# Second stage of layer two: the centre and weight products of two steps issued in one run

## The chip, the cores and the metric

The kernel runs on one core of a Trainium2 chip. The metric is the device time of one execution in microseconds (us), lower is better. All engine names are those of the profile: PE is TensorE's matmul, PEld its weight load, DVE is VectorE, ACT is ScalarE, POOL is GpSimd and SP is SyncE, which here only issues DMAs.

## The reference, cut to what matters

The input has 4 images of 64 channels and 256 x 256 pixels. Layer one is a gated convolution with a blockwise Fourier part. Layer two runs a linear state-space recurrence over all pixels, once row by row and once column by column, each with its own weights:

```
fx  = layer_norm(x, ln1_g, ln1_b)
h   = s5_scan(fx, ...)              # forward and backward scan, complex state
x   = gelu(h) + fx
fx2 = layer_norm(x, ln2_g, ln2_b)
y   = fx2 @ ff_enc.T @ ff_dec.T + fx2
out = fusion_w @ concat(y_h, y_v) + fusion_b
```

The change touches only the part from `gelu(h)` on. A second layer norm is needed there: its mean is taken out by a product with a centring matrix, its variance comes from the squares of that, and the product with the weight matrix (in which `ff_enc`, `ff_dec` and the fusion are folded) is scaled afterwards by the reciprocal deviation.

## The kernel before, in words

The work on an image is layer one, then for layer two each direction in turn (`d` = 1, then `d` = 0) a first stage (`pa_...`) and a second stage (`pb_...`). So the second stage runs 8 times. It goes through 16 groups (`NG`) of 4 steps, 64 steps `m` in all (`M`), each over a tile of 128 x 512. Each engine has its own written-out program with its own loop over `m`, and semaphores tie them together.

In one step TensorE does, in this order (`pb_pe`, the loop at its end):

- `first(m)`: 12 matmuls (L1776), into the PSUM bank of the step.
- in the second step of a group (m % 4 == 1) `var`: 32 short matmuls (L1350) that add up the squares of the group before.
- `bc(m - 6)`: one matmul (L1821) that spreads the reciprocal deviations of six steps ago (`LAG`) over the partitions. It alternates between banks 3 and 5, and so waits for the `norm` of two steps before it.
- `second(m)`: 6 matmuls (L1789) from the state `XP`, into the bank of `first`. In the first step of a group it waits for the new `XP` (semaphore `X`). There is one `XP`, so VectorE can write it only when the last `second` of the old group has ended.
- `center(m - 1)`: two fp32 products with `ctq` (L1800) into bank 2 and two with `Wq` (L1803) into bank 6 or 7, each on a 64 x 64 quadrant of the array, so that the four run side by side. Each is recorded as two passes.

ScalarE (`pb_act`) does the Gelu of the step from PSUM to `X2` (L1865), then the square of the centred values (L1871) and the copy of the weight product into `tW` (L1878). In m % 4 == 1 it also takes the square root of the variances (L1854), with two table loads around it, and in `d` = 0 it puts out rows together (L1753).

VectorE (`pb_dve`) does `deviations_b` in m % 4 == 1 (L1340 to L1345: reciprocal and the tile `RD` that `bc` reads), then `add(m)` (L1922: fx times gain plus Gelu, into `X2`, the operand of `center`), in m % 4 == 3 `parts` (L1908 and L1911: the new `XP`), then `norm(m - 6)` (L1929: the spread deviations times `tW`), then `scan` of the next group in m % 4 == 0 (L1899 and four tiny operations) and `rotate` in m % 4 == 1 and 2 (L1719, L1720, L1722).

GpSimd (`fin_v` L1731, `fin_h` L1741) adds each normed tile to the tile `av` or `ah` from memory. It starts when `norm` has ended.

SyncE issues all loads and stores in one queue. Near the end of `d` = 0 it already issues the first loads of the next image, the tiles `XT` among them.

Of the kernel before, what the change touches and what calls it, by code (L numbers as in the profile page):

```python
# [7 lines left out]
ALU = mybir.AluOpType  # L8
ACT = mybir.ActivationFunctionType
# [5 lines left out]
NG = 16  # L15
# [3 lines left out]
M = 4 * NG  # L19

PARTS = ((0, 0), (0, 1), (1, 0))
LAG = 6
NW = 8
# [87 lines left out]
def build(nc, a, NB):  # L111
# [34 lines left out]
    g1 = at("g1", [128, 2])  # L146
# [143 lines left out]
    ah = [at(f"ah{i}", [128, 2, 1024]) for i in range(2)]  # L290
    oh = at("oh", [128, 8, 256])
    XT = [at(f"XT{i}", [128, 512]) for i in range(3)]

    ps = [nc.alloc_psum_tensor(f"ps{i}", [128, 512], F32) for i in range(6)]
    ps67 = nc.alloc_psum_tensor("ps6", [128, 2, 512], F32)
# [1336 lines left out]
    def pb_sp(e, b, d):  # L1632
        f = phase(b, d)

        def load(n):
            e.wait_ge(sem["yd"], M * f + 4 * (n - 2) + 4)
            e.dma_start(fq[n % 2][1][:].rearrange("p a b -> p (a b)").bitcast(F32), fl_d[b, d, order[n]]
                        ).then_inc(sem[f"fl_in{n % 2}"], 16)
            e.wait_ge(sem["x2"], M * f + 4 * (n - 2) + 4)
            e.dma_start(fi[n % 2][:].rearrange("p a b -> p (a b)"), fx_d[b, d, order[n]]).then_inc(sem[f"fi_in{n % 2}"], 16)  # L1640

        def load_v(n):
            if n >= 2:
                e.wait_ge(sem[f"avs{n % 2}"], 16 * (8 * b + (n - 2) // 2 + 1))
            for p, hf in ((0, slice(64, 128)), (1, slice(0, 64))):
                e.dma_start(av[n % 2][hf].rearrange("c v h w -> c (v h w)"),
                            x1v_d[b, order[n], p].rearrange("c v h w -> c (v h w)")).then_inc(sem[f"av{n % 2}"], 16)

        def load_h(n):
            g = order[n]  # L1650
            for p in range(2):
                if n >= 2:
                    e.wait_ge(sem["il"], M * b + 4 * (n - 2) + 2 * p + 2)
                for v, hf in ((0, slice(64, 128)), (1, slice(0, 64))):
                    e.dma_start(ah[n % 2][hf, p, :].rearrange("c (k r) -> c k r", k=16),
                                acc_d[b, :, 1 - p, :, v, 8 * g:8 * g + 8, :].rearrange("k c h w -> c k (h w)")
                                ).then_inc(sem[f"ah{n % 2}"], 16)

        e.wait_ge(sem["bm"], 32 * (f + 1))
        for p in range(2):  # L1660
            e.dma_start(Cwr[:, p, :].bitcast(F32), kc_d[d, p, :, 1024:2048]).then_inc(sem["kC"], 16)
        e.wait_ge(sem["t"], M * (f + 1))
        e.dma_start(TBo[:].rearrange("p a b -> p (a b)"), tb_d[d, :, 1024:2048]).then_inc(sem["kTo"], 16)
        if d:
            load_v(0)
            load_v(1)
        else:
            for k in range(2):
                e.wait_ge(sem[f"avs{k}"], 16 * 8 * (b + 1))
            load_h(0)  # L1670
            load_h(1)
        for n in range(NG + 1 if d else NG + 2):
            if 2 <= n + 2 < NG:
                load(n + 2)
            if n == NG - 1:
                if d:
                    ahead_a(e, b, 0)
                elif b + 1 < NB:
                    ahead_0(e, b + 1)
            if d and n:  # L1680
                g = order[n - 1]
                e.wait_ge(sem["finv"], M * b + 4 * n)
                e.dma_start(acc_d[b, g].rearrange("p c v h w -> (p c) (v h w)"),
                            av[(n - 1) % 2][:].rearrange("p v h w -> p (v h w)")).then_inc(sem[f"avs{(n - 1) % 2}"], 16)
                if n + 1 < NG:
                    load_v(n + 1)
            if not d and n >= 2:
                if n < NG:
                    load_h(n)
                if n == NG - 1 and b + 1 < NB:  # L1690
                    load_xt(e, b + 1, 1)
                    load_raw(e, b + 1, 1)
                    load_xt(e, b + 1, 2)
                    load_raw(e, b + 1, 2)
                if n < NG or b + 1 == NB:
                    store_rows(e, b, n - 2)
                elif n == NG:
                    for t in range(3):
                        load_h_rows(e, b + 1, t)
        if b == NB - 1 and not d:  # L1700
            e.wait_ge(sem["ost"], 32 * NG * NB)
# [53 lines left out]
    def pb_pe(e, b, d):  # L1755
        f = phase(b, d)

        def bank(m):
            return ps[{2: 3, 3: 5}.get(m, m % 2)]

        def first(m):
            n, s = divmod(m, 4)
# [29 lines left out]

        def center(m):
            e.wait_ge(sem["x2"], M * f + m + 1)
            if m:
                e.wait_ge(sem["sr"], M * f + m)
            if m >= 2:
                e.wait_ge(sem["tw"], M * f + m - 1)
            for hf in (slice(0, 64), slice(64, 128)):
                ins = e.matmul(ps[2][hf, :], ctq[hf, hf], X2[m % 2][hf, :], start=True, stop=True)  # L1800
            ins.then_inc(sem["cc"], 1)
            for hf, other in ((slice(0, 64), slice(64, 128)), (slice(64, 128), slice(0, 64))):
                ins = e.matmul(ps[6 + m % 2][other, :], Wq[hf, hf], X2[m % 2][hf, :], start=True, stop=True)  # L1803
            ins.then_inc(sem["w"], 1)

        def var(n):
# [6 lines left out]
        def bc(m):  # L1813
            n, s = divmod(m, 4)
            if s == 0:
                e.wait_ge(sem["rsb"], NG * f + n + 1)
            if m >= 2:
                e.wait_ge(sem["n2"], M * f + m - 1)
            else:
                e.wait_ge(sem["gl"], M * f + m + 3)  # L1820
            e.matmul(ps[3 + 2 * (m % 2)][:], Bc[:, 512 + 128 * s:640 + 128 * s], RD[:], start=True,  # L1821
                     stop=True).then_inc(sem["bd"], 1)

        for m in range(4):
# [1 line left out]
        for m in range(M + LAG):  # L1826
            if 4 <= m < M:
                first(m)
            if m >= 5 and m % 4 == 1 and m <= M + 1:
                var(m // 4 - 1)  # L1830
            if m >= LAG:
                bc(m - LAG)
            if m < M:
                second(m)
            if 1 <= m <= M:
                center(m - 1)

    def pb_act(e, b, d):
# [9 lines left out]
        for m in range(M + 2 if d else M + 9):  # L1848
# [11 lines left out]
                    p1(e, b + 1, 0)  # L1860
            if m < M:
                e.wait_ge(sem["y"], M * f + m + 1)
                if m >= 2:
                    e.wait_ge(sem["w"], M * f + m - 1)
                e.activation(X2[m % 2][:], ps[{2: 3, 3: 5}.get(m, m % 2)][:], ACT.Gelu_apprx_tanh, bias=cD[:, 4 * d + s:4 * d + s + 1]  # L1865
                             ).then_inc(sem["gl"], 1)
            if 1 <= m <= M:
                e.wait_ge(sem["cc"], M * f + m)
                if m >= 5:
                    e.wait_ge(sem["va"], M * f + m - 4)  # L1870
                e.activation(sr[:, (m - 1) % 4, :], ps[2][:], ACT.Square, bias=cC[:, d:d + 1]).then_inc(sem["sr"], 1)  # L1871
                e.wait_ge(sem["w"], M * f + m)
                if m - 1 >= NW:
                    if d:
                        e.wait_ge(sem["finv"], M * b + m - NW)
                    else:
                        e.wait_ge(sem["finh"], M * b + m - NW)
                e.activation(tW[:, (m - 1) % NW, :], ps[6 + (m - 1) % 2][:], ACT.Identity, bias=cW[:, d:d + 1]  # L1878
                             ).then_inc(sem["tw"], 1)
            if s == 1 and n:  # L1880
                for i in range(4):
                    part(n + 1, i)
# [5 lines left out]
    def pb_dve(e, own, b, d):  # L1888
# [25 lines left out]
        def add(m):  # L1914
            n, s = divmod(m, 4)
            e.wait_ge(sem["gl"], M * f + m + 1)
            if s == 0:
                if n >= 2:
                    fi_there(e, f, n)
                else:  # L1920
                    e.wait_ge(sem["nn"], M * (f + 1))
            e.scalar_tensor_tensor(X2[m % 2][:], fi[n % 2][:, s, :], g1[:, d:d + 1], X2[m % 2][:], ALU.mult, ALU.add  # L1922
                                   ).then_inc(sem["x2"], 1)

        def norm(m):
            e.wait_ge(sem["bd"], M * f + m + 1)
            e.wait_ge(sem["tw"], M * f + m + 1)
            t = tW[:, m % NW, :]
            e.tensor_tensor(t, ps[3 + 2 * (m % 2)][:], t, ALU.mult).then_inc(sem["n2"], 1)  # L1929

        e.wait_ge(sem["badd"], NG * (f + 1))
        e.wait_ge(sem["baddd"], f + 1)
# [4 lines left out]
        for m in range(M + 8):  # L1937
            n, s = divmod(m, 4)
            if s == 1 and 1 <= n <= NG:
                deviations_b(e, own, f, n - 1, "se", NG * f + n, "rsb")  # L1940
            if m < M:
                add(m)
                if s == 3 and n + 1 < NG:
                    parts(n + 1)
            if m >= LAG and m - LAG < M:
                norm(m - LAG)
            if s == 0 and n + 1 < NG:
                scan(n + 1)
            if s in (1, 2) and n + 1 < NG:
# [151 lines left out]
```

## Time and profile before

| | |
|---|---|
| time, median of 3 runs | 9187.77 us (9186.68 to 9197.3) |
| time of the profiled execution | 9189.68 us |
| its span | 9187.9 us |
| mean granted TensorE clock | 0.968 |
| PE busy | 8467.4 us, 92% |
| DVE busy | 8000.4 us, 87% |
| ACT busy | 5173.3 us, 56% |
| POOL busy | 1604.8 us, 17% |

The profile records one execution. Busy shares are means over very different stages, so what sets the pace of the second stage has to be read from a stretch inside it. The second stages start at about 1493 us for the first image and end at about 9163 us for the last one; the stretches used here lie in the last two images. Matmuls are pipelined: a matmul of 512 columns is recorded with some 0.39 us, but the next one starts some 0.23 us after it.

### The profile page before, as it was taken

To read this page: it belongs to the slowest core of one execution; us is meant where nothing else is said; L and a number is where in the kernel's file an instruction comes from. 1 tells how busy PE (TensorE), PEld (TensorE's weight loads), DVE (VectorE), ACT (ScalarE), POOL (GpSimd) and SP (SyncE) were. 2 spreads that over 40 slices of the span, in tenths; PEclk is the share of its full clock that TensorE was granted. 3 is DMA by queue.
4 is the path that set the end of the run, shared out by engine and by line. 5 is a ranking of instruction groups with operands and counts; after the bars stand their busy time and mean duration, and the time that the engine had idled before them with its cause. 6 is when DMAs were issued, how large, how long until landed. Compare 5 with 4: busy or idle time off the path is not lost. (4 is left out here: it accounts for less than half of the span.)

```text
span 9187.9 us, 202861 instructions
## 1 busy us (share of the span) xinstructions
PE 8467.4 (92%) x82258; PEld 5525.6 (60%) x82258; DVE 8000.4 (87%) x11203; ACT 5173.3 (56%) x8027; POOL 1604.8 (17%) x1834
## 2 busy tenths in 40 slices
PE   0899989999899998998989999899998999899998
PEld 0566655656566664665656666565565666556565
DVE  7799988888799998879869999887887999898886
ACT  0455555576655556556765554656675555555666
POOL 0000003333300001232320000223341000023333
PEclk9899999999999998999999999999999999999999
DMA  4789876585688887557569887846667878765855
GB/s 113 173 189 197 188 195 205 175 259 152 169 188 192 188 196 224 165 179 240 168 166 196 190 191 167 256 157 213 197 178 158 179 171 179 178 208 182 258 150 156
DMA packets 1370028, 1719.03 MB, mean 187 GB/s; under 512 B 849788, under 2 KB 1081356, under 8 KB 1283852
## 3 DMA queue, kind: packets, MB, share of 16 engines
q1 hardware_dynamic: 1369100, 1706.04, 72.3%
q8 instruction: 657, 10.76, 0.5%
q14 instruction: 271, 2.22, 0.1%
HBM read 852.77 MB, written 514.86 MB: 149 GB/s over the span
## 5 line engine op out<-in xcount | busy, mean ns | idle before, releaser
L1181 DVE SCALAR_TENSOR_TENSOR F<-U,LW,F 106x512 f32<-106x512 f32 x2048 | 1537.2, 751 | 63.5
L1776 PE MATMUL ps<-fp,Dwr 128*128 128x512 f32 x6144 | 1548.8, 401 | 1.6 <-DVE tt L1544 1.6
L1776 PEld LDWEIGHTS ps<-fp,Dwr 128*128 128x128 f32 x6144 | 1115.2, 188 | 617.6 <-ACT x L1865 289.6
L1048 ACT ACTIVATE xr<-P 64x1024 fp32r<-64x1024 f32 x512 | 542.9, 1060 | 780.7 <-issue 770.6
L1865 ACT ACTIVATE x<-ps,cst 128x512 f32<-128x512 f32 x512 | 351.8, 687 | 1038.7 <-PE ps L1789 1034.2
L871 PE MATMUL ps<-P,WP 128*128 128x512 f32 x3072 | 859.9, 416 | 52.6 <-DMA H<-P 50.9
L1789 PE MATMUL ps<-XP,Cwr 128*128 128x512 f32 x3072 | 805.5, 399 | 82.2 <-DVE XP L1911 82.2
L871 PE MATMUL ps<-H,WP 128*128 128x512 f32 x3072 | 819.9, 402 | 0.0
L871 PEld LDWEIGHTS ps<-P,WP 128*128 128x128 f32 x3072 | 567.0, 191 | 391.5 <-issue 206.9
L1922 DVE SCALAR_TENSOR_TENSOR x<-fx,g,x 128x512 f32<-128x512 f32 x512 | 382.9, 748 | 467.3 <-ACT x L1865 467.0
L1424 PE MATMUL ps<-fp,Bwr 128*128 128x512 f32 x3072 | 774.9, 403 | 0.4 <-DVE tt L1544 0.3
L1741 POOL TENSOR_TENSOR ah<-tW,ah 128x256 f32<-128x256 f32 x512 | 584.4, 1167 | 992.2 <-DVE tW L1929 991.6
L1789 PEld LDWEIGHTS ps<-XP,Cwr 128*128 128x128 f32 x3072 | 585.0, 192 | 229.5 <-issue 96.7
L1424 PEld LDWEIGHTS ps<-fp,Bwr 128*128 128x128 f32 x3072 | 581.7, 193 | 218.7 <-issue 98.1
L1098 POOL TENSOR_SCALAR xo<-xo 64x512 f32<-64x512 f32 x4 | 6.0, 1500 | 4042.0 <-DVE xo L1206 4042.0
L871 PEld LDWEIGHTS ps<-H,WP 128*128 128x128 f32 x3072 | 577.7, 188 | 156.3 <-issue 1.9
L1731 POOL TENSOR_TENSOR av<-tW,av 128x512 f32<-128x512 f32 x256 | 473.5, 1855 | 1101.5 <-DVE tW L1929 1101.5
L1800 PE MATMUL ps<-x,ctq 64*64 64x512 f32 x2048 | 551.0, 615 | 10.2 <-DVE x L1922 10.0
L1803 PE MATMUL ps<-x,Wq 64*64 64x512 f32 x2048 | 551.0, 615 | 0.0
L1004 ACT ACTIVATE xh<-ps 128x504 f32<-128x504 f32 x256 | 151.1, 590 | 703.7 <-PE ps L820 703.5
L1157 DVE TENSOR_TENSOR Z<-ps,LW 128x680 f32<-128x680 f32 x512 | 441.4, 862 | 96.4 <-PE ps L835 88.5
L1462 ACT ACTIVATE sq<-ps,gn 128x512 f32<-128x512 f32 x512 | 350.1, 684 | 222.8 <-PE ps L1383 222.8
(302 smaller groups left out, 16726.8 us busy)
## 6 DMA issues: line engine op xcount, KB each, us to landing
H<-P SPq DMA_DIRECT2D x512, 585.0 KB, 7.4
raw<-x SPq DMA_DIRECT2D x240, 640.0 KB, 9.5
fx_d<-fx SPq DMA_DIRECT2D x112, 1024.0 KB, 6.6
fl_d<-fp SPq DMA_DIRECT2D x112, 1024.0 KB, 6.9
fp<-fl_d SPq DMA_DIRECT2D x112, 1024.0 KB, 6.7
fx<-fx_d SPq DMA_DIRECT2D x112, 1024.0 KB, 5.4
XT<-xT SPq DMA_DIRECT2D x256, 256.0 KB, 7.5
x1h_d<-xo SPq DMA_DIRECT2D x256, 256.0 KB, 9.2
```

What stands on the lines that cost most here:

```text
L871: e.matmul(ps[2 + i][:], w(pw_, W_CONV + 128 * j, 128), m, start=(j == 0 and pw_ == 0 and px == 0), stop=False)
L1048: ins = e.activation(xr[t % 2][hf], src, ACT.Copy)
L1157: e.tensor_tensor(Z[t % 2][:, 4 * h:4 * h + 4, :].rearrange("q (j p) h -> q j (p h)", j=2), ps67[:, :, 0:2 * HID], Wt.unsqueeze(1).to_broa ...
L1181: ins = e.scalar_tensor_tensor(o, u, wd[0:106, i:i + 1], o, ALU.mult, ALU.add)
L1424: ins = e.matmul(o[:], Bwr[:, w, 128 * (2 * s + j):128 * (2 * s + j) + 128], fp[g % 2][x][:, s, :], start=(s == 0 and w == 0 and x == 0), ...
L1731: e.tensor_tensor(o, t, o, ALU.add).then_inc(sem["finv"], 1)
L1741: ins = e.tensor_tensor(o, t, o, ALU.add)
L1776: ins = e.matmul(bank(m)[:], Dwr[:, w, c:c + 128], fq[n % 2][x][:, s2, :], start=(s2 == 0 and w == 0 and x == 0), stop=False)
L1789: ins = e.matmul(bank(m)[:], Cwr[:, w, c:c + 128], XP[x][:, j, :], start=False, stop=(j == 1 and w == 1))
L1800: ins = e.matmul(ps[2][hf, :], ctq[hf, hf], X2[m % 2][hf, :], start=True, stop=True)
L1803: ins = e.matmul(ps[6 + m % 2][other, :], Wq[hf, hf], X2[m % 2][hf, :], start=True, stop=True)
L1922: e.scalar_tensor_tensor(X2[m % 2][:], fi[n % 2][:, s, :], g1[:, d:d + 1], X2[m % 2][:], ALU.mult, ALU.add).then_inc(sem["x2"], 1)
```

## The change

`center(m)` is no longer called in every step. In every second step it is called twice in a row, after `second(m)`, for m - 2 and m - 1. For this the centred values get two banks (2 and 5), `X2` gets four buffers (the two new ones share their memory with `XT1` and `XT2`), and `bc` keeps only bank 3, so that it waits for the `norm` of the step before it. ScalarE does its squares and copies of two steps in a row as well. VectorE calls `norm` ahead of `add` and `parts`, no longer behind them. SyncE loads the `XT` tiles that share memory one iteration later, behind a wait for the last weight product.

```diff
+    X2 += XT[1:3]
...
                 if n == NG - 1 and b + 1 < NB:
+                    load_raw(e, b + 1, 1)
+                    load_raw(e, b + 1, 2)
+                if n == NG and b + 1 < NB:
+                    e.wait_ge(sem["w"], M * (f + 1))
                     load_xt(e, b + 1, 1)
-                    load_raw(e, b + 1, 1)
                     load_xt(e, b + 1, 2)
-                    load_raw(e, b + 1, 2)
...
         def bank(m):
-            return ps[{2: 3, 3: 5}.get(m, m % 2)]
+            return ps[{2: 3, 3: 4}.get(m, m % 2)]
...
         def center(m):
             e.wait_ge(sem["x2"], M * f + m + 1)
-            if m:
-                e.wait_ge(sem["sr"], M * f + m)
             if m >= 2:
+                e.wait_ge(sem["sr"], M * f + m - 1)
                 e.wait_ge(sem["tw"], M * f + m - 1)
             for hf in (slice(0, 64), slice(64, 128)):
-                ins = e.matmul(ps[2][hf, :], ctq[hf, hf], X2[m % 2][hf, :], start=True, stop=True)
+                ins = e.matmul(ps[(2, 5)[m % 2]][hf, :], ctq[hf, hf], X2[m % 4][hf, :], start=True, stop=True)
...
         def bc(m):
-            if m >= 2:
-                e.wait_ge(sem["n2"], M * f + m - 1)
+            if m:
+                e.wait_ge(sem["n2"], M * f + m)
             else:
-                e.wait_ge(sem["gl"], M * f + m + 3)
-            e.matmul(ps[3 + 2 * (m % 2)][:], Bc[:, 512 + 128 * s:640 + 128 * s], RD[:], start=True,
+                e.wait_ge(sem["gl"], M * f + 3)
+            e.matmul(ps[3][:], Bc[:, 512 + 128 * s:640 + 128 * s], RD[:], start=True,
                      stop=True).then_inc(sem["bd"], 1)
...
-            if 1 <= m <= M:
+            if m % 2 == 0 and 2 <= m <= M:
+                center(m - 2)
                 center(m - 1)
...
     def pb_act(e, b, d):
-            if 1 <= m <= M:
-                e.wait_ge(sem["cc"], M * f + m)
+            for c in (m - 2, m - 1) if m % 2 == 0 and 2 <= m <= M else ():
+                e.wait_ge(sem["cc"], M * f + c + 1)
...
     def pb_dve(e, own, b, d):
+            if m >= LAG and m - LAG < M:
+                norm(m - LAG)
             if m < M:
                 add(m)
                 if s == 3 and n + 1 < NG:
                     parts(n + 1)
-            if m >= LAG and m - LAG < M:
-                norm(m - LAG)
```

## Rows read from the trace of the kernel before

**Rows 1.** Chain that ended last, one group: start, us, what.
```profile
8404.00 2.98 PE ps L1776 x12
...
8408.57 0.58 PE ps L1800 x2
...
8409.59 2.97 PE ps L1776 x12
...
8423.73 1.01 PE ps L1350 x32
...
8427.57 0.66 PE ps L1776 x2
```

**Rows 2.** Timeline of PE, runs with no change of shape: start, us, engine, what.
```profile
7460.03 1.04 PE L898 MATMUL ps<-raw,FR 64*64 64x512 f32 x4
7460.89 1.05 PE L951 MATMUL ps<-F,LW 42*64 42x512 f32 x4
...
8169.18 5.60 PE L1776 MATMUL ps<-fp,Dwr 128*128 128x512 f32 x24
```

**Rows 3.** Timeline of ACT and DVE from the last `second` of a group.
```profile
8414.20 0.69 ACT L1865 ACTIVATE x<-ps,cst 128x512 f32<-128x512 f32 x1 [3.31 <-PE ps L1789]
...
8414.92 0.75 DVE L1922 SCALAR_TENSOR_TENSOR x<-fx,g,x 128x512 f32<-128x512 f32 x1 [0.24 <-ACT x L1865]
...
8416.26 1.29 DVE L1911 TENSOR_TENSOR XP<-tq,XP 128x512 fp32r<-128x512 f32 x2
```

**Rows 4.** Timeline where `second` waits for `XP`, early in a stage.
```profile
8204.85 1.28 DVE L1911 TENSOR_TENSOR XP<-tq,XP 128x512 fp32r<-128x512 f32 x2
...
8206.18 1.66 PE L1789 MATMUL ps<-XP,Cwr 128*128 128x512 f32 x6 [0.41 <-DVE XP L1911]
...
8207.77 0.65 PE L1800 MATMUL ps<-x,ctq 64*64 64x512 f32 x2
```

**Rows 5.** Timeline of DVE beside POOL's final addition, in both directions.
```profile
8406.74 2.03 POOL L1731 TENSOR_TENSOR av<-tW,av 128x512 f32<-128x512 f32 x1 [6.72 <-DVE tW L1929]
...
8407.17 2.13 DVE L1720 TENSOR_TENSOR tq<-S,TBo 128x512 f32<-128x512 f32 x1
...
8992.30 1.80 POOL L1741 TENSOR_TENSOR ah<-tW,ah 128x256 f32<-128x256 f32 x1
...
8993.84 0.28 DVE L1616 SCALAR_TENSOR_TENSOR S<-S,e,tiny 64x1 f32<-64x1 f32 x1
```

**Rows 6.** Whole run by source line: count, duration in ns, min/median/max.
```profile
L1616 DVE SCALAR_TENSOR_TENSOR S<-S,e,tiny x128: 218/219/276, 1508.5 to 9112.4; 64x1 f32<-64x1 f32 x128
...
L1720 DVE TENSOR_TENSOR tq<-S,TBo x256: 681/1373/2159, 1509.6 to 9121.3; 128x512 f32<-128x512 f32 x128
...
L1922 DVE SCALAR_TENSOR_TENSOR x<-fx,g,x x512: 736/751/754, 1518.9 to 9148.4; 128x512 f32<-128x512 f32 x171
...
L1731 POOL TENSOR_TENSOR av<-tW,av x256: 1567/1660/2692, 1546.8 to 8570.7; 128x512 f32<-128x512 f32 x128
```

**Rows 7.** Timeline from `var` to VectorE's `add`, and that `add` mid-stage.
```profile
8211.74 1.08 PE L1350 MATMUL ps<-sr,En 128*32 128x128 f32 x32
...
8215.59 0.74 DVE L1922 SCALAR_TENSOR_TENSOR x<-fx,g,x 128x512 f32<-128x512 f32 x1
...
8405.31 0.74 DVE L1922 SCALAR_TENSOR_TENSOR x<-fx,g,x 128x512 f32<-128x512 f32 x1
```

**Rows 8.** Timeline of PE and DVE at the end of a second stage.
```profile
8563.91 1.40 PE L1821 MATMUL ps<-RD,Bc 128*128 128x512 f32 x2 [3.76 <-DVE RD L1345]
...
8566.81 1.99 PE L1383 MATMUL ps<-xin,Mb 64*64 64x512 f32 x8
...
8563.77 0.68 DVE L1929 TENSOR_TENSOR tW<-ps,tW 128x512 f32<-128x512 f32 x1
...
8564.74 1.29 DVE L1929 TENSOR_TENSOR tW<-ps,tW 128x512 f32<-128x512 f32 x2 [0.29 <-PE ps L1821]
```

**Rows 9.** Timeline of SP's queue at the turn to another image.
```profile
6948.56 42.34 SPq L719 DMA_DIRECT2D H<-P  x6
```

More of the change, by code:

```diff
@@ L1794, in center @@
             e.wait_ge(sem["x2"], M * f + m + 1)
-            if m:
-                e.wait_ge(sem["sr"], M * f + m)
             if m >= 2:
+                e.wait_ge(sem["sr"], M * f + m - 1)
                 e.wait_ge(sem["tw"], M * f + m - 1)
             for hf in (slice(0, 64), slice(64, 128)):
-                ins = e.matmul(ps[2][hf, :], ctq[hf, hf], X2[m % 2][hf, :], start=True, stop=True)
+                ins = e.matmul(ps[(2, 5)[m % 2]][hf, :], ctq[hf, hf], X2[m % 4][hf, :], start=True, stop=True)
             ins.then_inc(sem["cc"], 1)
             for hf, other in ((slice(0, 64), slice(64, 128)), (slice(64, 128), slice(0, 64))):
-                ins = e.matmul(ps[6 + m % 2][other, :], Wq[hf, hf], X2[m % 2][hf, :], start=True, stop=True)
+                ins = e.matmul(ps[6 + m % 2][other, :], Wq[hf, hf], X2[m % 4][hf, :], start=True, stop=True)
             ins.then_inc(sem["w"], 1)
@@ L1862, in pb_act @@
                 e.wait_ge(sem["y"], M * f + m + 1)
-                if m >= 2:
-                    e.wait_ge(sem["w"], M * f + m - 1)
-                e.activation(X2[m % 2][:], ps[{2: 3, 3: 5}.get(m, m % 2)][:], ACT.Gelu_apprx_tanh, bias=cD[:, 4 * d + s:4 * d + s + 1]
+                if m >= 4:
+                    e.wait_ge(sem["w"], M * f + m - 3)
+                e.activation(X2[m % 4][:], ps[{2: 3, 3: 4}.get(m, m % 2)][:], ACT.Gelu_apprx_tanh, bias=cD[:, 4 * d + s:4 * d + s + 1]
                              ).then_inc(sem["gl"], 1)
-            if 1 <= m <= M:
-                e.wait_ge(sem["cc"], M * f + m)
[L1869 to L1873, printed above, removed]
+            for c in (m - 2, m - 1) if m % 2 == 0 and 2 <= m <= M else ():
+                e.wait_ge(sem["cc"], M * f + c + 1)
+                if c >= 4:
+                    e.wait_ge(sem["va"], M * f + c - 3)
+                e.activation(sr[:, c % 4, :], ps[(2, 5)[c % 2]][:], ACT.Square, bias=cC[:, d:d + 1]).then_inc(sem["sr"], 1)
+                e.wait_ge(sem["w"], M * f + c + 1)
+                if c >= NW:
                     if d:
-                        e.wait_ge(sem["finv"], M * b + m - NW)
+                        e.wait_ge(sem["finv"], M * b + c - NW + 1)
                     else:
-                        e.wait_ge(sem["finh"], M * b + m - NW)
-                e.activation(tW[:, (m - 1) % NW, :], ps[6 + (m - 1) % 2][:], ACT.Identity, bias=cW[:, d:d + 1]
-                             ).then_inc(sem["tw"], 1)
+                        e.wait_ge(sem["finh"], M * b + c - NW + 1)
+                e.activation(tW[:, c % NW, :], ps[6 + c % 2][:], ACT.Identity, bias=cW[:, d:d + 1]).then_inc(sem["tw"], 1)
             if s == 1 and n:
@@ L1921, in add @@
                     e.wait_ge(sem["nn"], M * (f + 1))
-            e.scalar_tensor_tensor(X2[m % 2][:], fi[n % 2][:, s, :], g1[:, d:d + 1], X2[m % 2][:], ALU.mult, ALU.add
+            e.scalar_tensor_tensor(X2[m % 4][:], fi[n % 2][:, s, :], g1[:, d:d + 1], X2[m % 4][:], ALU.mult, ALU.add
                                    ).then_inc(sem["x2"], 1)
@@ L1928, in norm @@
             t = tW[:, m % NW, :]
-            e.tensor_tensor(t, ps[3 + 2 * (m % 2)][:], t, ALU.mult).then_inc(sem["n2"], 1)
+            e.tensor_tensor(t, ps[3][:], t, ALU.mult).then_inc(sem["n2"], 1)
         e.wait_ge(sem["badd"], NG * (f + 1))
```

## Prediction

> **What bounds the kernel now.** I read the page first (PE is busy 92% and DVE 87%, so neither can be ruled out), then the list of waits, then the chain that ended last in a stretch in the middle of a second stage. There the chain consists of PE alone: each group of four steps takes 8427.57 - 8404.00 = 23.57 us, a plain step 8409.59 - 8404.00 = 5.59 us, and `center` 8409.59 - 8408.57 = 1.02 us of it [rows 1]. So a group is 4 x 5.59 + 1.21 us, the last for `var` and its surroundings. The reader should see that nothing outside PE appears in that chain, so what PE saves is saved, until something else comes late. Last I read the timeline of all engines in the same stretch, to find what is nearly late.
>
> **What PE saves.** A matmul with no change of shape around it costs (5.60 - 0.39) / 23 = 0.227 us [rows 2]. The 19 full-array matmuls of a step would be 4.32 us in one unbroken run; the step without `center` takes 4.57 us, and `center` itself 1.02 us, while a pair of fp32 passes of the same shape that follows another 64 x 64 product takes 7460.89 - 7460.03 = 0.86 us [rows 1, 2]. So going into the quadrant shape and back costs (4.57 - 4.32) + (1.02 - 0.86) = 0.41 us. Two `center` calls in one run have this once and not twice. I take 0.40 us for a pair. The bounds are 0.25 us (only the change on the side of `first` goes away) and 0.41 us. A group has two pairs: -0.80 us.
>
> **What becomes late: `XP`.** The pairs are issued in steps with even m, so after m % 4 == 3 no `center` stands between the last `second` of a group and the next group's `first`. It was the cover of a chain on other engines: that last `second` ends (8414.16), Gelu starts 8414.20, `add` 8414.92, `parts` ends 8417.55 [rows 3]. From end to end this is 3.39 us, and it can't begin sooner, since `XP` is single. Before, PE had `center`, `first` and `bc` meanwhile, 1.02 + 2.97 + 0.23 = 4.22 us. Now it has 13 matmuls, 13 x 0.227 = 2.95 us. Where `second` has to wait for `XP`, the following `center` starts 8207.77 - 8206.13 = 1.64 us after `parts` ended [rows 4]. So it would start 3.39 + 1.64 = 5.03 us after the last `second`, where an unbroken run brings it after 19 x 0.227 = 4.32 us, less 0.05 us of pipelining. The new stall is 0.76 us in each group (bounds 0.65 and 0.85). It eats the saving nearly whole: -0.04 us.
>
> **What is late next: `add` behind GpSimd.** `norm` now stands ahead of `add`, and GpSimd's final addition starts as soon as `norm` ends. The rows show that GpSimd's addition and a VectorE operation with two operands from SBUF exclude each other: L1720 takes 0.68 us alone, but 2.13 us when it starts inside the addition that began at 8406.74, so that it works as if it had begun 0.15 us before that addition's end [rows 5, 6]. Does this hold for `add`, a SCALAR_TENSOR_TENSOR? It never met an addition before (736 to 754 ns in all 512 cases), but a tiny operation of its kind took 0.28 us and not 0.22 where it started 0.26 us before the end of an addition (8994.10; 276 ns is also its maximum) [rows 5, 6]. I take it that `add` is held. The Trainium skill says the same in SBUF — State Buffer, section SBUF: two separate sides: the port pair that VectorE and GpSimd share is an exclusive lock, taken for a whole instruction by a VectorE operation with two SBUF inputs or by GpSimd, whoever starts first. The trace agrees for L1720 (2.13 against 0.68 us); for `add` the rule speaks against this change. By the sums below a group would be 24.33 us with it and 23.53 us without.
>
> Where are they in the critical step? Let z be the end of a group's first `second`. Then come two `center` (1.88 us) and `first` (2.97), so `var` starts at z + 4.85. VectorE gets through the deviations 8215.59 - 8211.74 = 3.85 us later [rows 7], at z + 8.70. From there to the end of the second `rotate` it was 8414.68 - 8405.31 = 9.37 us with the same operations in it [rows 3, 7] (the scan before it may get faster, since GpSimd has moved away from it, but it then waits for `var`). So `norm` of the last step runs from z + 18.07 to z + 18.75 and GpSimd's addition (1.66 us, [rows 6]) to z + 20.4. The last `second` ends three steps and `var` after z, that is 3 x 5.59 + 1.21 - 3 x 1.02 + 2 x 1.88 - 0.23 = 18.45 us; with Gelu, `add` could start at z + 19.2. It is held for about 1.1 us in this direction. In the other one there are two shorter additions for one, VectorE has less to wait for in `rotate`, and I expect 0.5 us. Mean: 0.80 us. Bounds: 0 (no hold, or the addition is over in time) and 1.5 us (`add` escapes, and `parts` is held). It goes in full into the stall of `second`.
>
> **A group**: 23.57 - 0.80 + 0.76 + 0.80 = 24.33 us, +0.76. There are 14 such groups in a stage (in the first, PE waits for VectorE anyway, and after the last no new `XP` is made) and 8 stages: 112 x 0.76 = +85 us.
>
> **The ends of a stage.** At the start, `center` of step 2 ran while PE would have waited for `XP` [rows 4]; now it follows: +0.86 us. One more pair near the end saves 0.40 us. At the end the last four `bc` follow each other; with one bank each waits for the `norm` before it. It was 8566.81 - 8563.91 = 2.90 us from the first of them to the next stage's product. Now the first goes at 8564.51 (end of the `norm` that starts at 8563.77, plus 0.06), and each further one 0.83 + 0.68 + 0.06 = 1.57 us later, so the next stage starts 0.60 + 3 x 1.57 + 0.70 - 2.90 = 3.1 us later [rows 8]. That is in full at the four turns between directions. At the turn to another image the copies H<-P wait for SyncE's queue until 6948.56 and PE for them [rows 9], and at the end of the kernel GpSimd, with 1.66 us an addition [rows 6] against 1.57 us from `norm` to `norm`, sets the pace: 1 us each is my estimate, four times. Sum: 8 x (0.86 - 0.40) + 4 x 3.1 + 4 x 1 = +20 us.
>
> **Costed at nothing.** The later `XT` loads: in SyncE's queue they stand ahead of H<-P as before, and the last weight product is done when the queue gets there. Were that cover gone, it would be a few us at three turns. The moved squares and copies on ScalarE (56% busy) end before `var`. The single bank of `bc` inside a group: each `norm` ends at least 0.8 us before its `bc`; without that margin each us late is paid once a group, 112 us. The second Gelu bank for step 3 only changes a number.
>
> **Sum.** 9189.68 (the profiled execution, 1.9 us above the median) + 85 + 20 = 9295, so 9293 us beside the median.
>
> **Rivals.** *The stall without the hold*: `add` is not held, or GpSimd is done in time. For it: no row shows `add` itself held. Against it: the tiny operation of the same kind. Then 112 x -0.04 + 20 = +16: 9204 us; with a saving of 0.25 us a pair +50: 9238 us. Chance 0.17. *The saving comes through* (faster): the wait for `XP` is hidden. It decides at the point where `parts` ends less than 2.6 us after the last `second`, for instance if Gelu and `add` cost PE nothing because `first` takes longer than I say; against it stand the 3.39 us read directly. Then 8 x 29 x -0.40 + 20 = -73: 9115 us; half of it 9150. Chance 0.10. *One bank for `bc` is too few*: VectorE, held more often by GpSimd, becomes the pace of a group, and `bc` waits for `norm` in mid-group. For it: DVE had only 0.24 us idle before `add` in the critical step [rows 3]. Then a group takes 25 us or more: 112 x 1.5 + 20 = +188: 9376 us. Chance 0.10. *The change does nothing that can be measured* is contained in the first rival's lower part.
>
> **Numbers.** My forecast has a chance of 0.63, and its own range is 9250 to 9330. A measurement of this kernel tells about 0.2% (18 us) from no change. Faster by more: 0.10. Within: 0.11, from the first rival. Slower by more: 0.79. The range for 8 in 10 goes down into the first rival and up to a hold of 1.5 us: 9197 to 9345.
>
> **What the profile after would show.** Right: PE's `second` in the first step of a group has idle time before it, released by L1911, some 1.5 us 14 times a stage; L1922 has a maximum near 1.5 to 2 us, no longer 754 ns; the scan L1899 loses its long cases (near 2.8 us); the group is near 24.3 us; two `center` in a row take 1.88 us. Wrong: if L1922 keeps its 0.75 us, the hold is wrong; if no idle time stands before `second`, the stall is; if a pair takes 2.04 us, the saving is; if `bc` has idle time released by L1929 in mid-group, the third rival is right.

## The result, and the profile after

The changed kernel takes 9299.12 us (median of 4 runs, 9296.88 to 9302.09) against 9190.8 us before in the same comparison (9186.68 to 9197.3): a ratio of 1.0116, 95% interval 1.01 to 1.0132. The forecast was 9293 us. The profiled execution took 9298.31 us, 108.6 us more than the one of before.

The page of the changed kernel, its engines and one of the costliest groups (line numbers have moved by one to three; behind the first bar stand busy us and mean ns of one, behind the second the idle time before and its releaser):

```profile
PE 8401.1 (90%) x82258; PEld 5561.6 (60%) x82258; DVE 7967.6 (86%) x11203; ACT 5148.8 (55%) x8027; POOL 1575.5 (17%) x1834
...
L1792 PE MATMUL ps<-XP,Cwr 128*128 128x512 f32 x3072 | 819.0, 404 | 237.4 <-DVE XP L1913 237.4
```

PE, VectorE, ScalarE and GpSimd are each busy for less time than before, and the kernel is slower: the time went into waiting. The lists of waits, first the kernel before, then the changed kernel twice (total us, number of waits, longest):

```profile
PE ps L1789 <- DVE XP L1911: 82.2, 16, 9.9
```

```profile
PE ps L1792 <- DVE XP L1913: 237.4, 128, 9.9
...
PE ps L1823 <- DVE tW L1931: 59.3, 32, 5.7
```

`second` stood idle for 237.4 us until VectorE had written `XP`, against 82.2 us before. The 112 new waits are 14 in each of the 8 stages.

The timeline of the second stage of the first direction, one critical step and what follows it:

```profile
8502.84 1.53 PE L1792 MATMUL ps<-XP,Cwr 128*128 128x512 f32 x6
...
8503.88 0.68 DVE L1931 TENSOR_TENSOR tW<-ps,tW 128x512 f32<-128x512 f32 x1
8504.21 2.89 PE L1779 MATMUL ps<-fp,Dwr 128*128 128x512 f32 x12
8504.41 0.69 ACT L1868 ACTIVATE XT<-ps,cst 128x512 f32<-128x512 f32 x1 [2.99 <-PE ps L1792]
8504.64 1.65 POOL L1734 TENSOR_TENSOR av<-tW,av 128x512 f32<-128x512 f32 x1 [2.55 <-DVE tW L1931]
8505.13 1.70 DVE L1924 SCALAR_TENSOR_TENSOR XT<-fx,g,XT 128x512 f32<-128x512 f32 x1 [0.57 <-ACT XT L1868]
8506.76 0.75 DVE L1910 CAST XP<-tq 128x512 fp32r<-128x512 f32 x2
...
8507.43 1.28 DVE L1913 TENSOR_TENSOR XP<-tq,XP 128x512 fp32r<-128x512 f32 x2
...
8508.76 1.66 PE L1792 MATMUL ps<-XP,Cwr 128*128 128x512 f32 x6 [1.44 <-DVE XP L1913]
```

Read it from the top. The last `second` of a group ends at 8504.37, and `first` follows with no `center` between. `norm` ended at 8504.56, so GpSimd's addition starts at 8504.64. `add` starts at 8505.13, inside it, and takes 1.70 us, where the kernel before had 0.75 [rows 3]. `parts` ends at 8508.71, and PE has been idle for 1.44 us when `second` goes on.

By source line, the two forms of `add` and the scan (duration in ns, min/median/max):

```profile
L1924 DVE SCALAR_TENSOR_TENSOR x<-fx,g,x x256: 741/751/754, 1520.5 to 9248.0; 128x512 f32<-128x512 f32 x128
L1924 DVE SCALAR_TENSOR_TENSOR XT<-fx,g,XT x256: 741/830/1729, 1527.2 to 9258.0; 128x512 f32<-128x512 f32 x128
...
L1901 DVE TENSOR_TENSOR_SCAN S<-RR,S x256: 1261/1276/1287, 1507.2 to 9217.2; 64x512 f32<-64x512 f32 x128
```

The form that writes the two new buffers is that of m % 4 == 2 and 3. Its maximum is 1729 ns, against 754 in [rows 6]. The scan has lost all its long cases, since GpSimd no longer works beside it; that gained nothing, because VectorE then waited for `var` and the square root after it (262.4 us in 128 waits, for 70.6 us in 24 before).

The starts of the waiting `second`, four groups apart, give the group. First direction, then second:

```profile
8337.52 1.66 PE L1792 MATMUL ps<-XP,Cwr 128*128 128x512 f32 x6 [1.47 <-DVE XP L1913]
...
8435.41 1.65 PE L1792 MATMUL ps<-XP,Cwr 128*128 128x512 f32 x6 [1.44 <-DVE XP L1913]
...
8945.44 1.65 PE L1792 MATMUL ps<-XP,Cwr 128*128 128x512 f32 x6 [1.17 <-DVE XP L1913]
...
9042.68 1.63 PE L1792 MATMUL ps<-XP,Cwr 128*128 128x512 f32 x6 [1.24 <-DVE XP L1913]
```

That is 97.89 / 4 = 24.47 us and 97.24 / 4 = 24.31 us, for 23.57 in [rows 1]. TensorE's granted clock was 1.00 of full speed in the group of [rows 1] (8404.00 to 8427.57) and in four groups of the changed kernel (8435.41 to 8533.30), so the clock has no part in the difference. In the second direction the hold sits elsewhere, in the last of these groups:

```profile
9038.65 2.16 POOL L1744 TENSOR_TENSOR ah<-tW,ah 128x256 f32<-128x256 f32 x2 [1.95 <-DVE tW L1931]
...
9039.25 0.83 DVE L1924 SCALAR_TENSOR_TENSOR XT<-fx,g,XT 128x512 f32<-128x512 f32 x1 [0.68 <-ACT XT L1868]
9040.00 1.43 DVE L1910 CAST XP<-tq 128x512 fp32r<-128x512 f32 x2
```

`add` slips in between the two additions with 0.08 us of delay, and then the CAST of `parts` takes 1.43 us instead of 0.75 while the second addition runs. The CAST has one operand in SBUF, not two. One CAST takes 0.42 us when nothing lies beside it, less than the 0.68 to 0.75 us of the operations with two operands on as many elements.

### The profile page after: what moved, and what is told of

The parts are those of the page before. It is cut to its first block and busy times, and to the rows that moved or that the text cites. A ratio compares the mean times of both kernels' runs of the same rounds, so it can differ in the third digit from the quotient of the medians.

```text
span 9296.5 us, 202840 instructions
## 1 busy us (share of the span) xinstructions
PE 8401.1 (90%) x82258; PEld 5561.6 (60%) x82258; DVE 7967.6 (86%) x11203; ACT 5148.8 (55%) x8027; POOL 1575.5 (17%) x1834
## 5 line engine op out<-in xcount | busy, mean ns | idle before, releaser
L1779 PE MATMUL ps<-fp,Dwr 128*128 128x512 f32 x6144 | 1511.1, 395 | 1.9 <-DVE tt L1545 1.9
L1779 PEld LDWEIGHTS ps<-fp,Dwr 128*128 128x128 f32 x6144 | 1134.5, 188 | 430.7 <-issue 194.9
L1792 PE MATMUL ps<-XP,Cwr 128*128 128x512 f32 x3072 | 819.0, 404 | 237.4 <-DVE XP L1913 237.4
L1744 POOL TENSOR_TENSOR ah<-tW,ah 128x256 f32<-128x256 f32 x512 | 562.0, 1124 | 1049.2 <-DVE tW L1931 1047.1
L1868 ACT ACTIVATE x<-ps,cst 128x512 f32<-128x512 f32 x256 | 176.1, 688 | 767.4 <-PE ps L1792 763.3
L1868 ACT ACTIVATE XT<-ps,cst 128x512 f32<-128x512 f32 x256 | 176.4, 689 | 480.8 <-PE ps L1792 480.8
L1149 DVE SCALAR_TENSOR_TENSOR P<-raw,ga,P 128x1300 fp32r<-128x1300 f32 x256 | 400.9, 1566 | 29.9 <-ACT P L1141 29.9
L1026 ACT ACTIVATE U<-ps,bu 106x390 f32<-106x390 f32 x512 | 271.7, 582 | 264.2 <-PE ps L887 264.2
```

The costliest lines, as they stand in the source:

```text
L1149: e.scalar_tensor_tensor(P[t % 2][1][:], raw[st % 3][:, :, 128 * dt:128 * dt + 130], nm, P[t % 2][0][:].bitcast(F32), ALU.add, ALU.subtrac ...
L1744: ins = e.tensor_tensor(o, t, o, ALU.add)
L1779: ins = e.matmul(bank(m)[:], Dwr[:, w, c:c + 128], fq[n % 2][x][:, s2, :], start=(s2 == 0 and w == 0 and x == 0), stop=False)
L1792: ins = e.matmul(bank(m)[:], Cwr[:, w, c:c + 128], XP[x][:, j, :], start=False, stop=(j == 1 and w == 1))
L1868: e.activation(X2[m % 4][:], ps[{2: 3, 3: 4}.get(m, m % 2)][:], ACT.Gelu_apprx_tanh, bias=cD[:, 4 * d + s:4 * d + s + 1]).then_inc(sem["gl ...
```

## The experiments

The runs of the kernel before in the same comparisons have medians of 9191.26 us (the first four experiments) and 9190.66 us (the last four). Groups are given for the first and the second direction.

**GpSimd's addition behind `parts`** (on the changed kernel). GpSimd has one more wait, so that its addition does not lie beside `add` and `parts` in the critical step.

```diff
+    def fin_later(e, f, m):
+        k = (m + LAG) // 4
+        if m % 4 == 1 and k + 1 < NG:
+            e.wait_ge(sem["X"], NG * f + k + 2)
...
+        fin_later(e, phase(b, 1), m)
...
+        fin_later(e, phase(b, 0), m)
```

> The changed kernel, with one wait more on GpSimd: the final addition that follows the norm in m % 4 == 3 starts only when parts has written the new XP (semaphore X). So nothing of GpSimd lies beside add and parts there. Theory (the hold by GpSimd is a term of its own, 0.96 us in the first direction and 0.78 in the second): add keeps 0.75 us and the CAST 0.42, the idle time before second falls from 1.44 to about 0.5 us, the group goes from 24.47 and 24.31 us to 23.53, and the kernel from 9299 to about 9299 - 4 x 13 x 0.94 - 4 x 13 x 0.78 = 9210 us. Rival (VectorE is late by its own work, whatever GpSimd does): group and time stay, 9299 us.

Measured: 9206.47 us (9200.69 to 9211.14), ratio 1.0014 (1.0005 to 1.0023); groups of 23.52 us in both directions. The timeline of the critical step:

```profile
8429.61 0.75 DVE L1931 SCALAR_TENSOR_TENSOR XT<-fx,g,XT 128x512 f32<-128x512 f32 x1 [0.57 <-ACT XT L1875]
8430.28 0.75 DVE L1917 CAST XP<-tq 128x512 fp32r<-128x512 f32 x2
8430.95 1.29 DVE L1920 TENSOR_TENSOR XP<-tq,XP 128x512 fp32r<-128x512 f32 x2
8432.29 1.65 PE L1799 MATMUL ps<-XP,Cwr 128*128 128x512 f32 x6 [0.49 <-DVE XP L1920]
8432.38 3.21 POOL L1740 TENSOR_TENSOR av<-tW,av 128x512 f32<-128x512 f32 x2 [5.82 <-DVE XP L1920]
```

`add` is back at 0.75 us and the idle time fell from 1.44 to 0.49 us, with GpSimd's work only moved. That one wait more takes 93 us off shows the hold. The 0.49 us that stay, and a group that is no faster than before, show the other term: the cover. (The idle time is less than this term costs the group, since it is counted from the recorded end of `bc`, 0.39 us after its start, where an unbroken run goes on after 0.23; and a `second` that had to wait takes 1.59 us to `center`, another 1.46.) The moved additions now lie beside the next `add`, which takes 1.43 us at 8434.70, but no group pays for that.

**One pair in a group** (on the changed kernel). A single `center` stands again behind the last `second` of a group.

```diff
+    def run(m):
+        return {2: (m - 2, m - 1), 3: (m - 1,), 0: (m - 1,), 1: ()}[m % 4] if 1 < m <= M else ()
...
-            if m % 2 == 0 and 2 <= m <= M:
-                center(m - 2)
-                center(m - 1)
+            for c in run(m):
+                center(c)
...
     def pb_act(e, b, d):
-            for c in (m - 2, m - 1) if m % 2 == 0 and 2 <= m <= M else ():
+            for c in run(m):
```

> The changed kernel, with only one pair in a group: center(m-2) and center(m-1) in m % 4 == 2, one center each in m % 4 == 3 and 0, none in 1. So one center stands again between the last second of a group and the next first. Theory (a stall because the cover of 1.02 us is gone): the pair saves 0.40 us instead of 0.80, XP must be there after 4.22 - 0.07 us and is there after 3.39 + hold (0.96 or 0.78) us, with 0.44 us to spare before and so 0.3 to 0.5 us late: group 23.57 - 0.40 + 0.4 = 23.6 us, time about 9210 to 9225 us. Rival (the stall comes from running two steps' squares and copies together on ScalarE, which has the same work in m % 4 == 2 here): group above 24 us, time above 9250 us.

Measured: 9189.1 us (9183.25 to 9201.27), ratio 0.9997 (0.9988 to 1.0007); groups of 23.61 and 23.34 us. The first direction is as expected; the second is better, and the time is below the range that I gave. With one pair a group without any stall would take 23.57 - 0.40 = 23.17 us, so the groups are late by 0.44 and 0.17 us. The hold is 0.97 us in the first direction (`add` takes 1.72 us in the median, for 0.75) and 0.69 us in the second (two CASTs, 1.44 for 0.75): in both some 0.5 us of it was to spare, a little more than I had taken. The second direction accounts for about half of the 28 us by which the time lies below the middle of my range: 52 groups, each 0.26 us shorter than the 23.6 us I gave. The rest was not taken apart. The rival with ScalarE's work asked for groups above 24 us with one such pair, and is out for that pair; the version with both pairs and no stall, further down, speaks against it for two.

**The pairs at other steps** (on the changed kernel). The edit of the experiment before, with another table:

```diff
+        return {3: (m - 3, m - 2), 0: (m - 2, m - 1), 1: (), 2: ()}[m % 4] if 1 < m <= M else ()
```

> The changed kernel, with both pairs of a group at other steps: center(0) and center(1) of the group in m % 4 == 3, center(2) and center(3) in m % 4 == 0. PE has the same instructions and as few changes of shape, but a pair of 1.88 us now covers the making of XP. Theory: XP is wanted 1.88 + 2.97 + 0.23 = 5.08 us after the last second and is there after 3.39 us plus the hold; but VectorE, which still waits for var before its deviations, gets to its norm in m % 4 == 3 only 18.07 us after the first second of the group, while PE could end the last second after 16.3 us. So VectorE is next late by 1 to 2 us: group 23.2 to 23.8 us, time 9165 to 9225 us. Rival (any arrangement in pairs stalls as much as the changed kernel): 24.4 us and 9299 us. Rival (nothing else is late, the saving of 0.80 us comes through): 22.8 us, 9120 us.

Measured: 9283.1 us (9278.79 to 9285.17), ratio 1.0098 (1.0083 to 1.0113); groups of 24.33 and 24.11 us. This missed my range by 58 us at its upper end. The cover is there, and still PE waits 1.32 us for `XP`. The timeline tells why:

```profile
8480.00 0.95 DVE L1341 RECIPROCAL rs<-rs 128x128 f32<-128x128 f32 x1 [1.60 <-ACT rs L1859]
...
8491.58 0.69 DVE L1933 TENSOR_TENSOR tW<-ps,tW 128x512 f32<-128x512 f32 x1
8492.17 0.74 DVE L1926 SCALAR_TENSOR_TENSOR XT<-fx,g,XT 128x512 f32<-128x512 f32 x1
8492.34 2.11 POOL L1734 TENSOR_TENSOR av<-tW,av 128x512 f32<-128x512 f32 x1 [2.56 <-DVE tW L1933]
8492.83 2.23 DVE L1912 CAST XP<-tq 128x512 fp32r<-128x512 f32 x2
...
8496.32 1.65 PE L1795 MATMUL ps<-XP,Cwr 128*128 128x512 f32 x6 [1.32 <-DVE XP L1915]
```

VectorE waits 1.60 us for the square root after `var`, and from there to `XP` the trace shows no idle time of VectorE at all; what slows it is GpSimd. It arrives at `norm` after the Gelu is done, so `add` starts just ahead of GpSimd's addition and is not held; `parts` is: two CASTs take 2.23 us for 0.75. VectorE, and no longer PE, sets the pace. I had VectorE's chain right and left out that a hold of 1.5 us falls fully on a chain that is already the bound.

**`norm` ahead of `add`, alone** (on the kernel before).

```diff
+            if m >= LAG and m - LAG < M:
+                norm(m - LAG)
             if m < M:
                 add(m)
                 if s == 3 and n + 1 < NG:
                     parts(n + 1)
-            if m >= LAG and m - LAG < M:
-                norm(m - LAG)
```

> The kernel before, with one edit: norm ahead of add and parts on VectorE; everything else, the two banks of bc too, as before. Theory: GpSimd's addition falls on add or parts in m % 4 == 3 and delays XP by 0.7 to 1.0 us, of which 0.44 us was to spare: the group grows from 23.57 by 0.3 to 0.5 us, 9191 + 112 x 0.4 = 9225 to 9245 us, and L1922 gets a maximum near 1.7 us. In the other steps the hold only moves from one operation to the next. Rival (the order on VectorE is free, the loss in the changed kernel comes from the pairs alone): 9191 us, or less, since the scan is no longer held.

Measured: 9202.68 us (9197.39 to 9207.92), ratio 1.0011 (1.0002 to 1.002); groups of 23.73 and 23.63 us. The direction is right, the size a third of what I expected at most: 11 us for 34 to 54, and 0.16 and 0.06 us a group for 0.3 to 0.5. In the critical step:

```profile
8424.78 1.63 POOL L1731 TENSOR_TENSOR av<-tW,av 128x512 f32<-128x512 f32 x1 [2.55 <-DVE tW L1929]
...
8425.54 1.41 DVE L1922 SCALAR_TENSOR_TENSOR x<-fx,g,x 128x512 f32<-128x512 f32 x1 [0.84 <-ACT x L1865]
```

GpSimd's addition starts earlier before `add` than in the changed kernel (0.76 us against 0.49), so the hold is 0.66 us and not 0.95. In the second direction `add` takes 1.31 us in the median, a hold of 0.56 us. Each time 0.5 us of the hold costs nothing, as in the experiment with one pair: that much was to spare, where I had taken 0.44. The order on VectorE costs 0.16 and 0.06 us a group by itself; it is dear only together with the pairs, which took the spare time. The longest `add` of the trace takes 2.26 us, more than the 1.7 us that I expected, but in m % 4 == 2, where no group is longer for it.

**Two banks for the last four `bc`** (on the changed kernel).

```diff
-                e.wait_ge(sem["n2"], M * f + m)
+                e.wait_ge(sem["n2"], M * f + m - (m >= M - 4))
...
-            e.matmul(ps[3][:], Bc[:, 512 + 128 * s:640 + 128 * s], RD[:], start=True,
+            e.matmul(ps[5 if m in (M - 4, M - 2) else 3][:], Bc[:, 512 + 128 * s:640 + 128 * s], RD[:], start=True,
...
-            e.tensor_tensor(t, ps[3][:], t, ALU.mult).then_inc(sem["n2"], 1)
+            e.tensor_tensor(t, ps[5 if m in (M - 4, M - 2) else 3][:], t, ALU.mult).then_inc(sem["n2"], 1)
```

> The changed kernel, with the last four bc of a stage alternating between banks 5 and 3, so that each waits for the norm of two steps before, as in the kernel before; in the groups bc keeps one bank. Theory (the single bank costs 3.1 us at the end of a stage, in full at four turns and about 1 us at the other four): 9299 - 12 - 4 = 9283 us, groups unchanged at 24.47 and 24.31. Rival (the end of a stage is set by GpSimd or by loads): 9299 us.

Measured: 9283.45 us (9281.85 to 9285.33), ratio 1.0101 (1.0087 to 1.0115), groups unchanged: 15.7 us less than the changed kernel. The end of a stage, first in the changed kernel, then with two banks:

```profile
8660.00 0.77 PE L1823 MATMUL ps<-RD,Bc 128*128 128x512 f32 x1 [4.45 <-DVE tW L1931]
...
8661.55 0.80 PE L1823 MATMUL ps<-RD,Bc 128*128 128x512 f32 x1 [0.78 <-DVE tW L1931]
...
8664.71 0.80 PE L1823 MATMUL ps<-RD,Bc 128*128 128x512 f32 x1 [0.78 <-DVE tW L1931]
8665.43 1.99 PE L1384 MATMUL ps<-xin,Mb 64*64 64x512 f32 x8
```

```profile
8645.75 1.40 PE L1823 MATMUL ps<-RD,Bc 128*128 128x512 f32 x2 [3.76 <-DVE RD L1346]
8647.33 1.40 PE L1823 MATMUL ps<-RD,Bc 128*128 128x512 f32 x2 [0.18 <-DVE tW L1931]
8648.66 1.99 PE L1384 MATMUL ps<-xin,Mb 64*64 64x512 f32 x8
```

With one bank the `bc` follow each other every 1.57 us, and it is 5.43 us from the first of them to the next stage; with two it is 2.91 us, for 2.90 in [rows 8]. From the last `var` of a stage to the next stage's first product of `first`, the four turns between directions take 14.0 us more in the changed kernel than before, and 2.1 us more with two banks: 11.9 us, for the 12 expected. The 4 us of the other four turns are not shown: at the turns between images the traces of these kernels differ by up to 6 us, and the end of the kernel is the same with one bank and with two (36.6 us after the last `var`).

**The pairs at other steps, and GpSimd's addition behind `parts`.** The edits of the first and the third experiment together.

> The version with the pairs in m % 4 == 3 and 0 (9283 us, groups of 24.33 and 24.11 us, in which VectorE's chain sets the pace and the CAST of parts takes 2.23 us for two instead of 0.75), and GpSimd's addition after the norm in m % 4 == 3 starting only when XP is written. Theory (PE has its saving, and what held it was VectorE's chain, of which 1.5 us is GpSimd's hold of parts): group 24.3 - 1.5 = 22.8 to 23.0 us, near PE's floor of 22.77; time 9190 + 20 - 104 x 0.7 = about 9140 us. Rival (VectorE's chain is too long without the hold as well, since it waits for var): 23.5 us or more, 9200 us.

Measured: 9137.88 us (9133.57 to 9141.1), ratio 0.9943 (0.9927 to 0.9958); groups of 22.83 and 22.77 us. The chain that ended last is PE alone again:

```profile
8410.41 2.73 PE ps L1789 x12
...
8414.73 0.58 PE ps L1812 x2
...
8415.32 0.42 PE ps L1812 x2
...
8415.75 0.42 PE ps L1812 x2
...
8416.18 0.41 PE ps L1812 x2
...
8416.61 2.95 PE ps L1789 x12
```

Here the saving can be read pass by pass. The first pass of a run costs 0.58 us and every other 0.42, and `first` costs 2.95 us behind a `center` but 2.73 behind another full-array product: 0.16 + 0.22 = 0.38 us for each change of shape and back. The moved pairs have a price of their own that I did not look into: from the first product of a stage to its first `var` it is 45.0 us in the median, for 42.6 before and 43.5 in the changed kernel, some 20 us in all for 8 stages.

**The same with two banks for the last four `bc`.**

> The version with moved pairs and the late addition, and the last four bc of a stage on two banks as well. The parts should add up: 16 us less than the version without the last edit, about 9124 us, 0.7% under the kernel before. If the end of a stage is set by something else, it equals the version without the edit.

Measured: 9124.08 us (9119.12 to 9126.0), ratio 0.9927 (0.9914 to 0.9939). The parts add up (13.8 us less, for 16 expected), and this version beats both kernels. In its critical step nothing waits for long:

```profile
8431.46 0.74 DVE L1933 SCALAR_TENSOR_TENSOR XT<-fx,g,XT 128x512 f32<-128x512 f32 x1
8432.12 0.76 DVE L1919 CAST XP<-tq 128x512 fp32r<-128x512 f32 x2
8432.79 1.29 DVE L1922 TENSOR_TENSOR XP<-tq,XP 128x512 fp32r<-128x512 f32 x2
...
8434.14 1.21 PEld L1802 LDWEIGHTS ps<-XP,Cwr 128*128 128x128 f32 x6 [0.25 <-DVE XP L1922]
8434.16 1.60 PE L1802 MATMUL ps<-XP,Cwr 128*128 128x512 f32 x6
```

**The late `XT` loads, alone** (on the kernel before).

```diff
                 if n == NG - 1 and b + 1 < NB:
+                    load_raw(e, b + 1, 1)
+                    load_raw(e, b + 1, 2)
+                if n == NG and b + 1 < NB:
+                    e.wait_ge(sem["w"], M * (f + 1))
                     load_xt(e, b + 1, 1)
-                    load_raw(e, b + 1, 1)
                     load_xt(e, b + 1, 2)
-                    load_raw(e, b + 1, 2)
```

> The kernel before, with one edit: the loads of XT1 and XT2 for the next image come one iteration later, behind the wait for the last weight product, as in the changed kernel. I costed this at nothing: 9191 us, within 3 us. If the queue is held by the wait, or forward(1) waits for XT1, up to 10 us more at three turns: 9220 us.

Measured: 9192.07 us (9190.06 to 9202.35), ratio 1.0002 (0.9993 to 1.0011). No effect that can be measured, but not for the reason that I gave. SyncE's queue at the turn to an image:

```profile
6942.29 5.95 SPq L1629 DMA_DIRECT2D out<-oh  x2
6948.35 3.25 SPq L735 DMA_DIRECT2D XT<-xT  x2
6951.64 43.17 SPq L719 DMA_DIRECT2D H<-P  x6
```

The two loads now stand right ahead of the first H<-P and push it from 6948.56 [rows 9] to 6951.64. Before, they stood ahead of the stores, in time that the queue had to spare. PE's wait for the H copies went from 15.41, 15.15 and 14.99 us at the three turns to 16.69, 16.09 and 14.38: 1.6 us more in all, less than runs differ. Why the 3.1 us by which the copies are issued later reach PE only in part was not tried.

## Why the prediction was right

**What PE saves.** Taken as 0.40 us a pair. Two `center` in a row take 1.88 us in the changed kernel, as I had worked out, and the version with nothing late has groups of 22.77 us in the second direction, 0.80 under 23.57. Shown. The term on the side of the quadrants was read from layer one and came out right (0.16 us), the one on the side of `first` was 0.25 and is 0.22.

**The cover of `XP`.** Taken as a stall of 0.76 us a group. Without the hold the group is 23.52 us, so the stall is 23.52 - 23.57 + 0.80 = 0.75 us. Shown, by the first experiment and, beside it, by the moved pairs: where `center` covers the making of `XP` and GpSimd is out of the way, the stall is gone.

**The hold by GpSimd.** Taken as 1.1 and 0.5 us, 0.80 in the mean; it is 24.47 - 23.52 = 0.95 and 24.31 - 23.52 = 0.79 us, 0.87 in the mean. In the first direction the working held step by step. From the end of the first `second` of a group, at 8485.96 in the trace, `norm` came 17.92 us later (18.07 forecast), the last `second` ended at 18.41 (18.45), GpSimd's addition at 20.33 (20.4). What I had wrong was the second direction: I expected VectorE to be earlier there, and it was, but the hold only went from `add` to the CAST. The rule of the Trainium skill that I weighed (SBUF — State Buffer, section SBUF: two separate sides) holds for `add`: 1.70 against 0.75 us. The same section counts a VectorE operation in a mode that uses both ports as well; the CAST with its one SBUF operand, 1.43 us for two instead of 0.75, agrees with that, though no row tells the mode that it runs in.

**A group.** 24.33 us forecast, 24.47 and 24.31 measured. There are 14 full intervals from `var` to `var` in a stage, and a shorter last one. The first grew by 0.06 to 0.1 us only, since no `norm` comes before its `add`; the other 13 by 0.90 and 0.74 us: 4 x 13 x (0.90 + 0.74) = 85 us. I had 112 x 0.76 = 85 us: one group too many in each stage, each a little too cheap. That the two errors cancel to less than 1 us is luck, and so is the mean of the two holds in part: one was taken too high, the other too low.

**The ends.** 20 us forecast. Measured is 108.6 - 86 = 23 us, of which the two-bank experiment took off 15.7 us; I had 16.4 us for that part, of which the trace bears out the 12 at the turns between directions and not the 4 at the others. The start of a stage grew by 0.87 us in the median (0.86 forecast), and the last interval between two `var` shrank by 0.53 to 0.61 us (0.40 forecast).

**Costed at nothing.** The late loads cost nothing that can be measured, though the reason was wrong, as told above. In the changed kernel no `bc` waited for `norm` in mid-group: the 32 waits in the list are the last four `bc` of 8 stages. PE had no idle time over 0.1 us in any `var` but the last of a stage, so ScalarE's squares were in time. That rival, one bank too few, is out for the groups.

**The faster rival** asked for the wait for `XP` to be hidden. It was not in this change, but it can be: the version with moved pairs and late addition is that rival, 0.57% faster, and 0.73% with the two banks at the end.

## What to carry to other kernels

When work is drawn together to save changes of mode, look at what it covered where it stood: here the same pairs gave +1.2% or -0.6%, by the step at which they were issued and by one wait on GpSimd. An operation of GpSimd that reads and writes SBUF is not free for VectorE; place it where VectorE waits or takes an operand from PSUM (`norm` was never held), and not beside the few operations that another engine waits for. Where a chain is the bound, a delay counts in full; where it has time to spare, only what is left over.

## What the runs showed of the hardware

- GpSimd's addition delays a VectorE SCALAR_TENSOR_TENSOR with two SBUF operands (0.75 to 1.70 us) and a CAST with one (two of them 0.75 to 2.23 us); each ends as if the held operation had begun some 0.2 us before the end of the addition. Where VectorE was first, the addition took 2.1 us instead of 1.65.
- `norm`, with one operand in PSUM and one in SBUF, is not held: in the version with moved pairs and late addition 134 of them start inside an addition and take 0.69 us, the others 0.68.
- The scan, with 64 partitions, reached 2782 ns beside an addition in the kernel before and never more than 1287 ns in the changed one, where none lay beside it.
- Going from full-array fp32r products to four fp32 products on quadrants costs 0.16 us, and going back 0.22 us.
